# A six-layer post-norm decoder on one core: maxima by four heads in four banks, a gate with fewer steps, two value copies on ScalarE, and new orders of work

## The reference

```
x = LN(x + attention(x))                       # A1: 16 heads of 16, no biases
x = LN(x + cross_attention(x, ctx))            # A2: 77 keys, biases, output projection
x = LN(x + ffn(x))                             # F: ternary weights, 8-bit activations, gate * up, 1024 wide
x = LN(x + attention_with_rotation(x))         # A3: biases, output projection
x = LN(x + dtw_align(ctx, x))                  # E: time warping of 77 context rows onto 256 tokens
x = LN(x + gated_attention(x))                 # A4
```

```
h     = softmax(q_scaled k^T / 4) v                        # v = x Wv^T + bv
gates = softmax(h Wr^T + br)                               # 15 routed heads
mask  = one_hot(top_3(gates)) summed
sw    = softmax(h Ws^T + bs)                               # 2 shared weights
gate  = sum(concat(2*sw[0] * sw, 2*sw[1] * gates*mask*3))  # one number per token
out   = (h * gate) Wp^T + bp
```

## Time and profile before

| what | value |
|---|---|
| median of three runs | 6091.51 us |
| profiled execution, its own time | 6097.69 us |
| span of its instructions | 6095.9 us |
| TensorE / VectorE / ScalarE / GpSimd busy | 88% / 84% / 67% / 42% |
| mean granted TensorE clock | 0.967 |
| DMA, mean | 32 GB/s |

### The profile page before, as it was taken

How to read it: one execution, slowest core, us unless ns; L and a number is a source line. 1 busy time by engine, 2 the same in 40 slices (tenths; PEclk the granted TensorE clock), 3 DMA queues, 4 the chain that set the end, 5 groups by cost and what they waited for, 6 DMA issues and landing times. The chain is left out here.

```text
span 6095.9 us, 142938 instructions
## 1 busy us (share of the span) xinstructions
PE 5354.1 (88%) x54914; PEld 3828.5 (63%) x54914; DVE 5140.5 (84%) x12191; ACT 4107.7 (67%) x7345; POOL 2546.5 (42%) x2574
## 2 busy tenths in 40 slices
PE   6999999879999999969999999998049999999998
PEld 4666666646666666647777777776036666666665
DVE  6888888769999999977777777776859999999997
ACT  5777777658888888866666666665336666666665
POOL 0111111223333333334444444444037677667765
PEclk9999999989999999989999999999569999999999
DMA  1111111110000000010010101010100000000000
GB/s 53 48 43 48 43 48 43 43 32 29 26 28 29 29 29 28 27 41 21 28 33 29 33 29 33 29 32 25 34 22 25 25 29 25 25 25 29 26 25 22
DMA packets 140392, 194.40 MB, mean 32 GB/s; under 512 B 25808, under 2 KB 63696, under 8 KB 139344
## 3 DMA queue, kind: packets, MB, share of 16 engines
q1 hardware_dynamic: 139728, 185.26, 9.7%
HBM read 113.03 MB, written 72.18 MB: 30 GB/s over the span
## 5 line engine op out<-in xcount | busy, mean ns | idle before, releaser
L1008 ACT ACTIVATE Dpr<-pj 128x512 f32<-128x512 f32 x1024 | 528.7, 602 | 255.0 <-PE pj L802 254.6
L1175 DVE TENSOR_REDUCE Amp<-pj 128x2 f32<-128x512 f32 x1024 | 630.9, 685 | 65.0 <-PE pj L869 65.0
L1175 DVE TENSOR_REDUCE Cmp<-pj 128x2 f32<-128x512 f32 x1024 | 638.7, 682 | 49.7 <-PE pj L869 49.7
L1008 ACT ACTIVATE Apr<-pj 128x512 f32<-128x512 f32 x1024 | 522.1, 613 | 205.8 <-PE pj L802 205.8
L1008 ACT ACTIVATE Cpr<-pj 128x512 f32<-128x512 f32 x1024 | 528.8, 602 | 184.6 <-PE pj L802 184.6
L1175 DVE TENSOR_REDUCE Dmp<-pj 128x2 f32<-128x512 f32 x1024 | 644.8, 682 | 9.4 <-PE pj L869 7.2
L1109 POOL TENSOR_SCALAR Ave<-Amv 128x2 f32<-128x2 f32 x64 | 14.7, 229 | 981.2 <-DVE Amv L1242 981.2
L1109 POOL TENSOR_SCALAR Bve<-Bmv 128x2 f32<-128x2 f32 x128 | 29.3, 229 | 870.7 <-DVE Bmv L1242 870.7
L1081 POOL TENSOR_TENSOR Dnrm<-Dnrm,power 128x32 f32<-128x32 f32 x64 | 348.9, 5452 | 98.8 <-DVE Dnrm L1153 98.8
L1116 POOL TENSOR_SCALAR Dx<-Dres,Dmv,Drstd 128x256 f32<-128x256 f32 x256 | 312.6, 1230 | 28.9 <-POOL Drstd L1110 28.9
L1116 POOL TENSOR_SCALAR Bx<-Bres,Bmv,Brstd 128x256 f32<-128x256 f32 x256 | 312.7, 1230 | 28.6 <-POOL Brstd L1110 28.6
(11 more groups left out here) (311 smaller groups left out, 15426.9 us busy)
## 6 DMA issues: line engine op xcount, KB each, us to landing
Ax0T<-in_xT SPq DMA_DIRECT2D x64, 256.0 KB, 2.9
Ax<-in_x SPq DMA_DIRECT2D x64, 256.0 KB, 3.1
x_A_scratch<-Ax SPq DMA_DIRECT2D x64, 256.0 KB, 2.0
Bx<-x_A_scratch SPq DMA_DIRECT2D x64, 256.0 KB, 2.9
x_B_scratch<-Bx SPq DMA_DIRECT2D x64, 256.0 KB, 2.0
Cx<-x_B_scratch SPq DMA_DIRECT2D x64, 256.0 KB, 2.8
x_C_scratch<-Cqr SPq DMA_DIRECT2D x64, 256.0 KB, 2.0
Dx<-x_C_scratch SPq DMA_DIRECT2D x64, 256.0 KB
```

Of the source, the lines that this page charges most:

```text
L1008: ck.tell(act.activation(dst, ck.bank(step + (bank,))[0:n, :], ACT.Exp, scale=HD ** -0.5), "probs_ready", step)
L1175: ins = dve.tensor_reduce(dst, src, AX.X, ALU.max, negate=True)
```

## The change

- `max` steps now cover four heads with one bank each, in all four row blocks: eight matmuls and four reduces with 256 keys (four steps a sample), and 16 matmuls and four reduces with 77 keys (two steps). A step waits for all four banks first. The chains get shorter by as many steps.
- The gate no longer subtracts the maxima on VectorE. The maxima are taken negated and go in as the bias of the exponentials on ScalarE, which also gives the row sums: four small ACTIVATEs for one. The mixing has 10 VectorE instructions in place of 17, with fewer dependent steps. `oproj` of A4 waits for it by a semaphore of its own.
- In C and D the value's bias is no longer added to the values. ScalarE copies `v`, and adds the bias behind the attention, per feature, when it copies `oT` (two ACTIVATEs of 256 columns for one of 512). The bias is loaded as two columns in place of a broadcast row.
- The probabilities have four groups of buffers in A and B, three in C and D.
- A wait whose value the engine has already waited for on that semaphore is left out (in `Clock.wait`).
- All orders in `ORDER` are new.

```diff
-GROUPS = 3
+GROUPS = {"A": 4, "B": 4, "C": 3, "D": 3}
...
 def max_heads(att, i):
     if tiles_of(att) == 2:
-        c, e, pair = i // 4, i % 4 // 2, i % 2
-        return [[8 * c + 2 * g + e] for g in (2 * pair, 2 * pair + 1)]
-    return [[2 * g + 1, 2 * g] for g in (2 * i, 2 * i + 1)]
+        c, e = divmod(i, 2)
+        return [[8 * c + 2 * g + e] for g in range(4)]
+    return [[8 * i + 2 * g + 1, 8 * i + 2 * g] for g in range(4)]
...
     if kind == "max":
-        return [step + (0,), step + (1,)]
+        return [step + (g,) for g in range(4)]
...
-                    self.eng.wait_ge(sems[name], base[name] + counts.at[step, name, nth])
+                    value = base[name] + counts.at[step, name, nth]
+                    if value > self.reached.get(name, 0):
+                        self.reached[name] = value
+                        self.eng.wait_ge(sems[name], value)
...
-                        for i in range(2):
+                        for i in range(4):
                             ck.wait_bank_free(step + (i,))
...
+                    elif kind == "v" and att in ("A3", "A4"):
+                        ck.wait_bank_full(step)
+                        src = ck.bank(step)[:].rearrange("p (t h d) -> p t h d", t=QT, h=H)
+                        ck.tell(act.activation(vv[s][:, :, :, 0:HD], src, ACT.Copy), "v_ready", step)
+                    elif kind == "oT" and att in ("A3", "A4"):
+                        ck.wait_bank_full(step)
+                        for c in range(FC):
+                            ins = act.activation(atT[s][:, c, :], ck.bank(step)[:, c * S:(c + 1) * S], ACT.Identity,
+                                                 bias=tiles.col[att + "_bv"][:, c:c + 1])
+                        ck.tell(ins, "attnT_ready", step)
...
-                        ins = act.activation(ex[s][:], lg[s][:], ACT.Exp)
+                        for t in range(QT):
+                            for i, (low, high) in enumerate(((0, H - 1), (H - 1, H + 1))):
+                                ins = act.activation(ex[s][:, t, low:high], lg[s][:, t, low:high], ACT.Exp,
+                                                     bias=gs[s][:, i, t:t + 1], accum_out=gs[s][:, 2 + i, t:t + 1])
...
                         if att == "A4":
+                            ck.wait("mixed", ("mix", att, b))
...
-                        dve.tensor_reduce(gs[s][:, 0, :].unsqueeze(2), lg[s][:, :, 0:nr], AX.X, ALU.max)
-                        link(ck, dve.tensor_reduce(gs[s][:, 1, :].unsqueeze(2), lg[s][:, :, nr:H + 1], AX.X, ALU.max))
-                        dve.tensor_tensor(lg[s][:, :, 0:nr], lg[s][:, :, 0:nr],
-                                          gs[s][:, 0, :].unsqueeze(2).to_broadcast([P, QT, nr]), ALU.subtract)
-                        ck.tell(dve.tensor_tensor(lg[s][:, :, nr:H + 1], lg[s][:, :, nr:H + 1],
-                                                    gs[s][:, 1, :].unsqueeze(2).to_broadcast([P, QT, 2]), ALU.subtract),
-                                  "logits_ready", step)
+                        dve.tensor_reduce(gs[s][:, 0, :].unsqueeze(2), lg[s][:, :, 0:nr], AX.X, ALU.max, negate=True)
+                        ck.tell(dve.tensor_reduce(gs[s][:, 1, :].unsqueeze(2), lg[s][:, :, nr:H + 1], AX.X, ALU.max,
+                                                  negate=True), "logits_ready", step)
...
+                            ins = dve.max(top[s][:, t, :], ex[s][:, t, 0:nr])
+                        link(ck, ins)
+                        dve.reciprocal(gs[s][:, 5:7, :], gs[s][:, 2:4, :])
+                        link(ck, dve.tensor_reduce(gs[s][:, 4, :].unsqueeze(2), top[s][:, :, 0:ROUTED], AX.X, ALU.add))
+                        dve.tensor_tensor(gs[s][:, 7:9, :], ex[s][:, :, nr:H + 1].rearrange("p t i -> p i t"),
+                                          gs[s][:, 6:7, :].to_broadcast([P, 2, QT]), ALU.mult)
                         link(ck, dve.tensor_tensor(gs[s][:, 9, :], gs[s][:, 4, :], gs[s][:, 5, :], ALU.mult))
                         dve.tensor_tensor(gs[s][:, 10, :], gs[s][:, 7, :], gs[s][:, 8, :], ALU.add)
+                        link(ck, dve.scalar_tensor_tensor(out=gs[s][:, 11, :], in0=gs[s][:, 8, :], scalar=2.0 * ROUTED,
+                                                          in1=gs[s][:, 9, :], op0=ALU.mult, op1=ALU.mult))
+                        link(ck, dve.scalar_tensor_tensor(out=gs[s][:, 12, :], in0=gs[s][:, 7, :], scalar=2.0,
+                                                          in1=gs[s][:, 10, :], op0=ALU.mult, op1=ALU.mult))
+                        ck.tell(dve.tensor_tensor(gs[s][:, 15, :], gs[s][:, 11, :], gs[s][:, 12, :], ALU.add), "mixed", step)
```

More of the change, by code:

```diff
@@ L56 @@
 KEYS = {"A1": S, "A2": C, "A3": S, "A4": S}
-ALL_BIASES = ("A2_bq", "A2_bk", "A4_bk", "A2_bo", "A2_bv", "A3_bq", "A3_bk", "A3_bv", "A3_bo", "A4_bq", "A4_bv", "A4_bo")
+VALUE_BIASES = ("A3_bv", "A4_bv")
+ALL_BIASES = ("A2_bq", "A2_bk", "A4_bk", "A2_bo", "A2_bv", "A3_bq", "A3_bk", "A3_bo", "A4_bq", "A4_bo")
 SPLIT_BIASES = ("A2_bq", "A2_bk", "A4_bk")
@@ L127, in before_core @@
     if att == "A1":
-        steps = steps[:2] + maxima(att, b, 0)[:2] + steps[2:] + maxima(att, b, 0)[2:]
+        steps = steps[:2] + maxima(att, b, 0)[:1] + steps[2:] + maxima(att, b, 0)[1:]
     else:
@@ L145, in core @@
     if tiles_of(att) == 2:
-        return p[:1] + second[:2] + p[1:2] + second[2:] + shifted + p[2:3] + first + p[3:] + last
+        return p[:1] + second[:1] + p[1:2] + second[1:] + shifted + p[2:3] + first + p[3:] + last
     return p[:1] + second + shifted + p[1:] + first + last
@@ L305, in signals @@
             "gu": ["gated", "hid_ready"], "hq": ["dve_step"] * 3 + ["scale_ready"], "dist": ["dist_ready"],
-            "gate": ["logits_taken", "dve_step", "logits_ready"], "mix": ["dve_step"] * 7,
+            "gate": ["logits_taken", "logits_ready"], "mix": ["dve_step"] * 5 + ["mixed"],
         },
@@ L370, in __init__ @@
             if step[0] == "core":
-                self.group[step] = len(cores) % GROUPS
-                if len(cores) >= GROUPS:
-                    _, att, b, p = cores[-GROUPS]
+                self.group[step] = len(cores) % groups
+                if len(cores) >= groups:
+                    _, att, b, p = cores[-groups]
                     self.freed_by[step] = ("pv", att, b, octet_of(att, p))
@@ L534, in __init__ @@
                 self.split = {n: sb(n + "_split", [P, D], BF16, where) for n in SPLIT_BIASES if n.startswith(att)}
+                self.col = {n: sb(n + "_col", [P, FC], F32, where) for n in VALUE_BIASES if n.startswith(att)}
                 keys, nt = KEYS[att], tiles_of(att)
@@ L554, in __init__ @@
                 self.ve, self.rstd = each("ve", [P, QT, 2]), each("rstd", [P, QT, 2])
-                self.pr = [[sb(f"{phase}pr{i}_{g}", [P, QT, S], F32, where) for g in range(4)] for i in range(GROUPS)]
+                self.pr = [[sb(f"{phase}pr{i}_{g}", [P, QT, S], F32, where) for g in range(4)] for i in range(GROUPS[phase])]
                 if phase == "A":
@@ L622, in __init__ @@
                 def __init__(self, eng):
-                    self.eng, self.step, self.seen, self.s, self.turn = eng, None, {}, None, None
+                    self.eng, self.step, self.seen, self.s, self.turn, self.reached = eng, None, {}, None, None, {}
                 def move(self, step):
@@ L1154, in do @@
                                   "norms2", step)
-                    elif kind == "v":
+                    elif kind == "v" and att in ("A1", "A2"):
                         ck.wait_bank_full(step)
@@ L1353, in _ @@
                                   for n, t in tiles.row.items()]
+                        loads += [(t[:, c:c + 1].unsqueeze(1), io[n][None, c * P:(c + 1) * P].rearrange("o (p n) -> p o n", n=1))
+                                  for n, t in tiles.col.items() for c in range(FC)]
                         for dst, src in loads:
@@ L1377, in _ @@
                                                                          in1=out3[:], op0=ALU.mult, op1=ALU.add))
-                counts = Counts(lines)
+                counts = Counts(lines, GROUPS[phase])
                 with ExitStack() as blocks:
```

76 lines of the change are left out of this document (32 added, 44 removed).

## The result

The changed kernel took 6141.62 us (median of 4 runs, 6138.59 to 6157.23), the kernel before 6092.19 (4 runs, 6087.66 to 6099.28). The ratio is 1.0085, 95% interval 1.0066 to 1.0105: slower by 0.85%, where I had forecast 5996 and faster.

A forecast was written before the change was run, and what follows sets the result against it. Each phase was taken as bound by its loop's period over 64 samples, no engine alone. A +38, B 0, C -38, D -96 and setup +1 made -95 us: 6097.69 to 6003, as median 5996; range 5885 to 6080.

The forecast's parts named there:

- B's: Phase B: VectorE's steps make 22.1 of the 22.17 us period, the change removes nothing; 0, ends -0.1 and +0.8 a sample.
- A: Phase A: the new order puts waits in a row, period 17.93 to 18.5 us, +0.6 a sample, +38 us.
- Rival 1: Phase A gains too: period 17.3, -40 us instead of +38, so 5918 us; chance 0.22.
- C: Phase C: period 23.39 to 22.8 us by a walk of the new order, -0.6 a sample, -38 us.
- "-0.6 at most" of the maxima: Phase C: maxima in fours save TensorE two short steps a sample, -0.6 us at most.
- D: Phase D: period 24.31 to 22.8 us by a walk of the new order, -1.5 a sample, -96 us.
- VectorE's relief of 3.3 us a sample: Phase D: VectorE loses 1.0 us in the gate, 1.7 in the mixing and 0.6 for the value copy.
- The exponentials with row sums: Phase D, ScalarE: four small exponentials replace one of 34 elements, taken as 0.25 us each; only latency.
- Rival 2: The VectorE-GpSimd port lock goes along into D's mixing: D at 24.6, +19 us instead of -96, total 6111; chance 0.08.
- the prediction's sentence on the rule: Phase D: by the port-lock rule one 0.8 us wait stays in the mixing, 0.3 reaching the period, 19 us less gain.
- Rival 3: All phases: each maxima step waiting for four free banks loses 0.25 us, 224 us in all, so 6220; chance 0.07.
- Rival 4: Phase D: VectorE's relief goes unused as TensorE is 93% busy, D -0.5 only: 6060 or about 6090; chance 0.11.

The follow-up runs named there:

- base_later: The changed kernel, but in B GpSimd makes the residual base two samples ahead, away from VectorE's quantisation steps: 6041.11 us (0.9905).
- max_first: On top of base_later, VectorE's first maxima step of B goes ahead of the second hidden quantisation: 6015.34 us (0.9859).
- b_new2: The changed kernel with B's maxima again by two banks a step, two steps side by side in the new order: 6138.53 us (1.0059).
- b_values: The changed kernel with A and B entirely as before, but B's values too copied out by ScalarE: 5969.09 us (0.9788).

## Why the prediction was wrong, step by step

- **The step that failed is B's**: "The change takes nothing off it (same reduces, same links), so no order gains more than 0.1; it can lose, as 16 matmuls now wait for four banks. I take 0; ends -0.1 and +0.8". It measured +2.25 us a sample, +140 us with its filling, and even the far end was short. "same links" was wrong: I summed VectorE's steps with their durations of before and did not walk GpSimd's order beside the new one of VectorE. base_later shows 1.71 of it to be GpSimd's add over fq with the clock that goes with it, max_first 0.38 to be the maxima behind the hidden quantisation; 0.16 stays open. Counted in rounds at full clock it is 0.87 for the add, 0.21 for the maxima, 1.0 for the clock, and the same 0.16. The cause that I named for a loss, four banks, is worth nothing here (b_new2), though the sign that I gave for it, B slower than 22.6, came true.
- **A** 18.5 forecast, 18.45 measured. Most of the links that I walked hold (walked and measured): core2 to core3 3.85 and 3.66, core0 to pv1 1.9 and 1.81, pv1 to core1 1.86 and 1.86, core1 to norm0 1.96 and 1.81. Two are off and cancel: core3 to core0 3.8 and 4.41, norm0 by q to core2 5.27 and 4.9. TensorE's wait before norm0 is put down to ScalarE's probabilities, 0.45 at 711.30. It is the order's doing (18.47 with two banks). Rival 1 is out.
- **C** 22.8 forecast, 23.07 measured. The walk holds to 0.1 as far as core2 (17.8 walked, 17.87 measured from core3); the last link, by pv0 and k back to core3, took 5.2 for 5.0. The values' move was the gain, as I had it; the "-0.6 at most" of the maxima was nothing.
- **D** 22.8 forecast, 22.70 measured: right in size, wrong in its reason. I had put the gain to VectorE's relief of 3.3 us a sample. It was 2.2 (929.12 to 900.27 of 1000, at 24.33 and 22.70 a sample), since one step of the mixing still waits for GpSimd, L1332 with 1016 ns. And the relief in the old order brings 0.24 (0.43 without the two long rounds); 1.55 (1.36) is the order. My walk held because it walked the order, not because of the sum ahead of it: from pv0 it had pv1 at 10.8, core1 at 12.7 and v at 14.6, and they came at 10.7, 12.6 and 14.6. Of the waits in it one was wrong: the maxima before v waited 0.52 us and not 0.1. I had VectorE near 85% and TensorE near 94% in D; they are at 90% and 98%.
- **The exponentials with row sums**: I took 0.25 each. They take 0.29 and a read of the sum behind each 0.19: four of them from 5212.65 to 5213.81, 1.16 us. VectorE had other work for that long, as I said, so it cost nothing.
- **Rival 2** (the lock goes along) was the right mechanism in the wrong phase. It did go along in D, and it came up in C too, where the last add of the rotation takes 1.55 us on average and 0.69 in the kernel before. One step of each, VectorE then GpSimd, in D and then in C:

```profile
5214.92 1.06 DVE L1332 TENSOR_TENSOR Dgs<-Dex,Dgs 128x4 f32<-128x4 f32 x1
5214.68 1.28 POOL L1110 TENSOR_TENSOR Dqr<-Dqr,qe_sp 128x512 f32<-128x512 f32 x1
...
3594.15 1.57 DVE L698 TENSOR_TENSOR Cqr<-Cqr,Ck 128x512 f32<-128x512 f32 x1
3594.13 1.04 POOL L1142 TENSOR_TENSOR Cq<-CxT 128x512 f32<-128x512 f32 x1 [1.35 <-ACT CxT L1037]
```

  So B, C and D each have one such wait of 0.9 to 1.0 us a sample. In C and D the periods came within 0.3 us of walks that hold no such wait, with TensorE 98% busy; only B paid, where VectorE's steps fill the round. By the prediction's sentence on the rule, one such wait in the mixing costs D 0.3 a sample; D's 22.70 shows no sign of it.
- **Rival 3** (four banks at once, 6220, on A, B, C and D) holds for 0.16 in D alone. **Rival 4** (relief unused) is true of the gate and the values in D, and hid behind the order's gain.
- The clock stood in no step. Its price, 56 us, is more than the whole difference of the two kernels (49 us).

## What to carry to other kernels

When a new order moves VectorE's work, walk GpSimd's queue beside it: a two-element VectorE step beside a GpSimd add of 1.26 us costs 1.2 us instead of 0.2. Where VectorE bounds the phase, moving the add away, even by an added wait, was worth more than a VectorE step taken off (in two different orders of B: 100 us in base_later, 5 in b_values). Look at the granted clock by round before summing durations, since one recurring wait on TensorE can be paid twice. Test a bundle by phase and by part: here one part (the order) carried most of the gain and all of the loss, and the one that the title names first (four banks) brought nothing.
